# Layer 3 of a graph and expert network: the first normalisation moves to ScalarE, the routing bias to TensorE, and two VectorE steps go

## The reference

```
dw = (weight > 0.01) * 0.01 - (weight < -0.01) * 0.01
x = x + relu(adj @ (layernorm(x) @ dw) + bias)
xf = layernorm(x).reshape(-1, 128)
logits = xf @ router_w.T + router_b          # 32 experts
idx = argmax(logits)
out = relu(relu(xf @ W1[idx] + b1[idx]) @ W2[idx] + b2[idx])
x = x + out
```

## Time and profile before

| what | value |
|---|---|
| median of 3 runs | 2202.75 us |
| lowest and highest | 2199.62, 2203.97 us |
| the profiled execution's own time | 2199.14 us |
| its span | 2197.4 us |
| this stage, first row of L1763 to the end of the last send | 1785.1 to 2000.6 us |
| busy shares of the span: TensorE, VectorE, ScalarE, GpSimd | 77%, 56%, 38%, 35% |
| mean granted clock of TensorE | 0.866 of full speed |

### The profile page before, as it was taken

One profiled execution on the slowest core, in us unless ns is written; L12 is line 12 of the kernel. 1 busy time (PEld: TensorE's weight loads), 2 busy tenths in 40 slices (PEclk: granted clock), 3 DMA queues, 4 the chain that ended last, 5 costly groups with the idle time before them and its releaser, 6 DMA issues. The chain is left out here.

```text
span 2197.4 us, 44487 instructions
## 1 busy us (share of the span) xinstructions
PE 1691.7 (77%) x13042; PEld 1410.7 (64%) x13042; DVE 1234.2 (56%) x4542; ACT 824.8 (38%) x2531; POOL 764.8 (35%) x1118
## 2 busy tenths in 40 slices
PE   5567999987649966777777779935999957872996
PEld 4555777765639964566666657725999945661663
DVE  5673333349856756688888855512222248862543
ACT  2333444433336642344444434302655523330000
POOL 3430000013326745200000027773554424543565
PEclk8888999998879985799999989967999967665887
DMA  2100000001014420000000021114777752203331
GB/s 70 57 29 8 1 1 1 1 13 34 28 33 130 124 57 0 1 0 0 0 0 0 0 71 48 48 52 129 207 208 206 206 141 81 64 23 66 98 79 46
DMA packets 156776, 129.84 MB, mean 59 GB/s; under 512 B 27852, under 2 KB 131055, under 8 KB 156610
## 3 DMA queue, kind: packets, MB, share of 16 engines
q1 hardware_dynamic: 136130, 99.30, 16.6%
q0 software_dynamic: 13568, 25.90, 3.5%
q10 hardware_dynamic: 6912, 2.65, 0.6%
HBM read 96.51 MB, written 33.35 MB: 59 GB/s over the span
## 5 line engine op out<-in xcount | busy, mean ns | idle before, releaser
L1429 ACT ACTIVATE FEAT<-BANKS,EXP 128x128 f32<-128x128 f32 x544 | 155.0, 368 | 181.4 <-PE BANKS L1406 181.4
L1047 ACT ACTIVATE EXP<-BANKS,NEGMAX 128x128 f32<-128x128 f32 x512 | 139.0, 383 | 191.5 <-DVE NEGMAX L1059 191.5
L195 PE MATMUL BANKS<-ident,WA 128*128 128x128 f32 x256 | 62.8, 392 | 163.2 <-DVE WA L189 163.1
L1360 POOL DMA_INDIRECT scratch_made<-FEAT x136 | 130.2, 958 | 147.8 <-DVE FEAT L1489 144.8
L195 PEld LDWEIGHTS BANKS<-ident,WA 128*128 128x128 f32 x256 | 42.9, 199 | 174.2 <-DVE WA L189 136.8
L412 PE MATMUL BANKS<-FEAT,ident 128*128 128x256 f32 x588 | 150.0, 383 | 0.0
L1489 DVE TENSOR_TENSOR FEAT<-BANKS,B2BC 128x128 f32<-128x128 f32 x136 | 39.7, 292 | 194.5 <-PE BANKS L1415 194.5
L1406 PE MATMUL BANKS<-FEAT 128*128 128x128 f32 x1088 | 146.3, 278 | 2.4 <-DMA FEAT<-in_L_ffn_W1p 1.2
L1415 PE MATMUL BANKS<-AUX,FEAT 128*128 x1088 | 143.9, 275 | 0.4 <-ACT FEAT L1429 0.4
L1074 DVE RECIPROCAL WD<-BANKS 128x256 f32<-128x256 f32 x64 | 112.5, 1758 | 55.4 <-PE BANKS L1018 55.4
L1162 POOL DMA_INDIRECT scratch_sent<-FEAT,POS x128 | 123.7, 966 | 40.6 <-issue 37.8
(11 more groups left out here) (361 smaller groups left out, 4556.4 us busy)
## 6 DMA issues: line engine op xcount, KB each, us to landing
FEAT<-in_L_ffn_W1p SPq DMA_DIRECT2D x136, 256.0 KB
EXP<-in_L_ffn_W SPq DMA_DIRECT2D x128, 128.0 KB, 2.1
FEAT<-scratch_sent SPq DMA_DIRECT2D x136, 64.5 KB
STAGE<-in_adj SPq DMA_DIRECT2D x32, 256.0 KB, 3.0
EXP<-scratch_made SPq DMA_DIRECT2D x32, 256.0 KB
FEAT<-scratch_sent SPq DMA_DIRECT2D x96, 65.5 KB, 1.9
X<-in_x SPq DMA_DIRECT2D x16, 256.0 KB, 3.3
scratch_sent<-NONE SPq DMA_DIRECT2D x48, 65.5 KB, 3.9
```

Of the source, the lines that this page charges most:

```text
L195: last = pe.transpose(tile(ps, k), tile(src, k), ident[:])
L1047: last = act.activation(tile(EXS[:, par], 4 * k + n), tile(PS[j], c), ACT.Exp, bias=NEGMAX[:, par, 4 * k + n:4 * k + n + 1])
L1360: pool.indirect_dma_start(out=made2, out_offset=bass.IndirectOffsetOnAxis(ap=XI_I[:, t % R_IN, H:ROW2], axis=0), in_=YO[:, t % R_OUT, :], ...
L1429: last = act.activation(tile(HR[:, t % R_H], c), tile(PS[2 + t % 2], c), ACT.Gelu, bias=BT[:, c, t:t + 1])
```

## The change

The first normalisation of the stage is computed by ScalarE as x times a scale plus a shift; VectorE makes only the shift, minus mean times inverse deviation, for the four graphs of the group in one small instruction (shift1, L1714 in the new file). The router bias is loaded as one row and put into the logits' bank by a one-row matmul, as the graph bias already is, and the four logits matmuls add to it. The search for the greatest logit and for its index read the bank itself, and the comparison reads the index as the unsigned integer that it is. The bank of the logits is free again only when the index search has run (s.idx), no longer when the copy has (s.lg). GpSimd's dev now waits until ScalarE has read the RS of two groups before.

```diff
-        rb3 = lb("rb3", [P, E3])
+        rbrow = lb("rbrow", [1, E3])
+        NB3 = lb("NB3", [P, 2, G])
-        LG3 = lb("LG3", [P, 2, G, E3])
-        IDXG3 = lb("IDXG3", [P, 2, G, 8])
...
-                sp.dma_start(rb3[:], a["L3_ffn_router_b"].partition_broadcast(P)).then_inc(s.w, 16)
+                sp.dma_start(rbrow[:], a["L3_ffn_router_b"].rearrange("(o h) -> o h", o=1)).then_inc(s.w, 16)
...
                 def dev(i):
+                    reused(pool, s.xn, i, 2)
                     inverse_deviation(pool, i, i % 2, MV, RS, s.mv, s.var, s.rstd)
...
                 def logits(i):
                     pe.wait_ge(s.f, i + 1)
-                    reused(pe, s.lg, i, 1)
-                    for k in range(G):
-                        last = pe.matmul(PS[5][:, k * E3:(k + 1) * E3], tile(WF[:, i % 2], k), rw3[:], start=True, stop=True)
+                    reused(pe, s.idx, i, 1)
+                    pe.matmul(PS[5][:, 0:G * E3].rearrange("p (g e) -> p g e", g=G), ones[0:1, :],
+                              rbrow[:].unsqueeze(1).to_broadcast([1, G, E3]), start=True, stop=False, skip_group_check=True)
+                    for k in range(G):
+                        last = pe.matmul(PS[5][:, k * E3:(k + 1) * E3], tile(WF[:, i % 2], k), rw3[:],
+                                         start=False, stop=(k == G - 1), skip_group_check=True)
                     last.then_inc(s.lg_ps, 1)
...
             @block.scalar
+                def norm(i):
+                    act.wait_ge(s.shift1, i + 1)
+                    reused(act, s.x_ps, i, 2)
+                    for k in range(G):
+                        last = act.activation(tile(WA[:, i % 2], k), cols(X, G * i + k, H), ACT.Identity,
+                                              scale=RS[:, i % 2, 1, k:k + 1], bias=NB3[:, i % 2, k:k + 1])
+                    last.then_inc(s.xn, 1)
...
-                in_turn(NG, [(1, xT), (1, support), (3, norm2), (3, feat)])
+                in_turn(NG, [(1, norm), (1, xT), (1, support), (3, norm2), (3, feat)])
...
-                def norm(i):
+                def shift1(i):
                     v.wait_ge(s.rstd, i + 1)
-                    reused(v, s.x_ps, i, 2)
-                    normalise(v, i, i % 2, WA, MV, RS, 1, s.xn)
+                    reused(v, s.xn, i, 2)
+                    v.scalar_tensor_tensor(NB3[:, i % 2, :], MV[:, i % 2, :, 0], -1.0, RS[:, i % 2, 1, :], ALU.mult, ALU.mult
+                                           ).then_inc(s.shift1, 1)
...
-                    v.tensor_tensor(LG3[:, par], PS[5][:, 0:G * E3].rearrange("p (g e) -> p g e", g=G),
-                                    rb3[:].unsqueeze(1).to_broadcast([P, G, E3]), ALU.add).then_inc(s.lg, 1)
-                    wait_apart(v, s.lg, i + 1)
-                    for k in range(G):
-                        last = v.max(TOP3[:, par, k, :], LG3[:, par, k, :])
+                    for k in range(G):
+                        last = v.max(TOP3[:, par, k, :], PS[5][:, k * E3:(k + 1) * E3])
...
-                        last = v.max_index(IDX3[:, par, k, :], TOP3[:, par, k, :], LG3[:, par, k, :])
+                        last = v.max_index(IDX3[:, par, k, :], TOP3[:, par, k, :], PS[5][:, k * E3:(k + 1) * E3])
...
-                    v.tensor_copy(IDXG3[:, par], IDX3[:, par]).then_inc(s.idf, 1)
-                    v.wait_ge(s.idf, i + 1)
                     reused(v, s.rk, i, 3)
                     v.tensor_tensor(HOT[:, ring], iota32[:].unsqueeze(1).to_broadcast([P, G, E3]),
-                                    IDXG3[:, par, :, 0].unsqueeze(2).to_broadcast([P, G, E3]), ALU.is_equal).then_inc(s.hot, 1)
+                                    IDX3[:, par, :, 0].unsqueeze(2).to_broadcast([P, G, E3]), ALU.is_equal).then_inc(s.hot, 1)
...
-                in_turn(NG, [(1, norm), (3, shift), (0, combine), (0, stats), (6, place), (5, choice), (2, add), (4, top)])
+                in_turn(NG, [(1, shift1), (3, shift), (0, combine), (0, stats), (6, place), (5, choice), (2, add), (4, top)])
```

More of the change, by code:

```diff
@@ L1497, in program @@
                        "lg_ps lg top idx idf hot ms car rk rb pp pf pos neg posw dw dws g1 ctab got0 got1 got2 half used blank "
-                       "sent0 sent1 sent2 sent3 sent4 sent5 sent6")
+                       "shift1 sent0 sent1 sent2 sent3 sent4 sent5 sent6")
         s_got = (s.got0, s.got1, s.got2)
```

## The result

| | before | changed |
|---|---|---|
| median of 4 runs | 2201.18 us | 2222.54 us |
| lowest and highest | 2193.48, 2203.97 | 2208.90, 2224.49 |
| profiled execution, span | 2197.4 us | 2220.4 us |
| the stage, first weight step to the last send's start | 214.6 us | 244.4 us |
| its 13 full turns, logits to logits | 150.9 us | 178.1 us |

The ratio is 1.0102, with a 95% interval of 1.0068 to 1.0137: slower by about 1%, and outside the forecast range (2192 to 2212). The two spans differ by 23.0 us: the stage is 29.8 us longer, and the parts before and after it were 2.3 and 4.5 us shorter in this execution.

What follows compares the result with a forecast made beforehand. VectorE bounds the short turns, TensorE the long ones. Terms +5.8 + 0.7 - 2.7 - 1.5 = +2.3 us gave 2205.0 on the median; less 3.1 for the clock, forecast 2202.0 us, range 2192 to 2212.

Steps and rivals of the forecast that it cites:

- the clock term: TensorE's clock level in the stage's turns: one long turn fewer, taken as a choice, -3.1 us.
- more long turns: Rival, from bias through rank to logits: each additional long turn costs 3.9 us, giving 2209 or 2213; chance 0.17.
- Less work on VectorE: VectorE's turn 1.54 us shorter, so TensorE's rank no longer waits for HOT in full turns: -2.7 us.
- The bias matmul: New one-row matmul on TensorE before the logits, 0.28 to 0.52 us each, 16 blocks, not hidden: +5.8 us.
- ScalarE's normalisation: Four normalisations on ScalarE, 1.65 us: covered in full turns, uncovered in the first group, +0.7 us.
- The drain: After the last conv, three searches and two choices on VectorE get shorter on the way to POS: -1.5 us.
- Searches that read the bank: VectorE's search reading PSUM: not charged, from -0.03 to +0.05 us an instruction, eight in a turn.

Runs made afterwards that it cites:

- e2: Kernel before with only the one-row routing-bias matmul and the search on the bank; 2304.8 us against 2283.5 before, ratio 1.0085.
- e1: Changed kernel without its routing-bias matmul: VectorE copies the logits with the bias and the search reads that copy; 2279.4 us against 2283.5 before, ratio 0.9957.
- e5: Changed kernel with the routing bias on 128 rows, graph bias still on one; 2177.5 us against 2197.7 before, ratio 0.9914.
- e9: Changed kernel with the graph bias on 128 rows, routing bias still on one; 2176.4 us against 2200.9 before, ratio 0.9874.
- e14: Changed kernel with its one-row routing-bias matmul moved behind support, into TensorE's wait for norm2; 2259.1 us against 2284.9 before, ratio 0.9950.
- e13: Changed kernel with the routing bias on 128 rows and that matmul issued twice; 2276.2 us against 2284.9 before, ratio 1.0036.
- e8: Changed kernel with an unused 512-column, 128-row matmul added behind support, in TensorE's wait for norm2; 2193.0 us against 2197.7 before, ratio 0.9958.
- e3: Kernel before with only the first normalisation moved to ScalarE; 2271.6 us against 2283.5 before, ratio 0.9931.
- e10: Kernel before with only the graph bias put on 128 rows; 2189.0 us against 2200.9 before, ratio 0.9937.
- e6: Changed kernel with both the routing bias and the graph bias on 128 rows; 2165.6 us against 2197.7 before, ratio 0.9845.
- e11: e6 with the routing bias issued behind support, in TensorE's wait for norm2; 2162.9 us against 2200.9 before, ratio 0.9825.
- e12: e6 with both biases issued behind support, in TensorE's wait for norm2; 2163.4 us against 2200.9 before, ratio 0.9825.

## Why the prediction was wrong

**The step that failed is the clock term.** The prediction chose one long turn fewer, -3.1 us, because "less waiting is likelier to keep the high level than to lose it". The opposite came: all 13 full turns took 13.0 to 14.4 us, and together grew from 150.9 to 178.1 us, +27.2. That alone is more than the whole difference of the two spans (23.0 us). The mean granted clock over the 120 us fell from 0.70 to 0.57. The cause is the one-row bias matmul: e2, which has it and the search on the bank, has the whole loss (243.3 us), e1, which has neither, has mostly turns of 10.0, and e5 and e9 keep the search and have 10.2. e5, e9 and e14 show when it does harm: as one-row work, in a turn that already has 512 one-row columns, and in the stretch of work and not in the wait. How much of that is its rows and how much its length, e13 leaves open.

The rival **more long turns** had the side and the place right ("two blocks of one-row work now stand in a turn that already failed to lift the clock"), at a chance of 0.17. It priced one or two more long turns, 2209 to 2213; no full turn stayed short, and it was 2222.5. Six of the 13 are of a kind that the prediction didn't have, 13.04 us at a clock of 0.63. The range ended at 2212 for that reason. The prediction's own rows were enough to ask the question: in the long turn, TensorE was held by nothing but its ring at 0.50, so the one-row blocks and their place were what a new one would add to.

**The Trainium skill's rule** (TensorE: Matmul & The Clock Gate, section Why this matters for your kernels) would have continuous work release the clock. The runs agree in part. e8, which fills about 1 us of the gap, raises the mean clock from 0.57 to 0.72. But e5 has the same wait of 2.22 us in each turn and TensorE is busy for a smaller share of it (8.00 us of 10.22, against 10.50 of 12.72 and 12.45 of 14.67), and it has 0.83.

Of the other terms:

- **Less work on VectorE**: right. Busy time in a turn fell from 9.9 to 8.6 us, in the whole kernel by 21 us against 23 forecast. The waits for HOT in the full turns (-2.7 us) are gone. e3 (0.9931) and e9 against e10 (12.6 us) show a gain as long as the clock holds.
- **The bias matmul**: right in kind, priced at less than half. It takes 0.41 and 0.73 us at the two levels, and not 0.28 and 0.52, and with the idle time before its weight load and the next it costs 0.61 and 1.02. A quarter of the 512-column matmul leaves out what doesn't scale with columns. Six of the 16 ran at the high level and ten at the low one, some 14 us in place of 5.8, by my estimate from these rows. In the 13 full turns it is some 11 us; with the waits of 2.7 us gone, some 19 of the 27.2 us are left to the clock level, by the same estimate.
- **ScalarE's normalisation**: right. L1663 takes 485 ns an instruction, the block 1.65 us, and no full turn waits for it. In the first group it delays the transposes: from the start of the combine ahead of them to theirs it was 6.40 us before and is 7.13 after, +0.73, where +0.7 was forecast.
- **The drain**: the gain on VectorE came, the drain still got longer. The last two gaps from logits to logits took 6.81 and 7.36 us before, and 7.97 and 7.77 after: +1.6 us, where -1.5 was forecast. In the last gap, at the low level in both, the way over VectorE from the end of the logits to rank fell by 0.6 us, as forecast, and the bias matmul, which the prediction had booked elsewhere, added its 1.02.
- **Searches that read the bank**: nearly free. MAX8 went from 181 to 186 ns, FIND_INDEX8 from 186 to 191, and the comparison with the integers from 297 to 288. By the Trainium skill (VectorE: DVE Perf Modes, section The TRN2 errata) each would take 65 ns more, 120 cycles in place of 58 at 0.96 GHz. These rows show 5 ns.

The sum of what is known: turns +27.2, first group +0.7, drain +1.6, which is 29.5 of the stage's 29.8 us. The bias matmul's cost is inside these. The 6.8 us that the rest of the kernel gave back in this execution are not explained by any run.

**What stays open.** No run says why the level falls or rises where it does. No run separates rows from length: e13 comes near it, but is still 0.17 us shorter a turn, and its ratio doesn't bear out what its trace says; for the graph bias there is no such run at all.

## What to carry to other kernels

When a stage's turns fall into a short and a long kind at two clock levels, its time is set by which kind comes, and a term of a few tenths of a microsecond on TensorE decides more by that than by its own length; so price such an edit for both patterns, all short and all long, and let the range hold both. Put a bias that TensorE adds on all 128 rows (bias over 128, everywhere ones) and not on one: with both biases so, 2198 us became 2166 (e6), where the changed kernel with both on one row went from 2201 to 2222. Try it also where TensorE waits anyway; e11 and e12 came to 2163 from 2201, a step further that is within the noise. After each such gain look which cover has become thin; here ScalarE's normalisation was the next.

## What the runs showed of the hardware that was not expected

- The granted clock was lower with bias matmuls on one row than with the same columns on 128 rows. Both biases changed so, with nothing else, raised its mean from 0.57 to 0.84 and took the stage from 244.4 to 183.9 us (changed and e6). The 128-row form is also shorter, so this isn't shown to be the rows alone.
- A one-row matmul of 128 columns between 128-row ones takes 0.41 us at the high level and 0.73 at the low one; on 128 rows 0.22 and 0.42 (e5, e13). With what stands before the weight loads, the one-row form lengthens TensorE's list by 0.61 and 1.02 us. With 512 columns the matmul itself is 1.05 and 2.00 us on one row, 0.86 and 1.71 on 128 (e6).
- Moving the routing bias's one-row matmul by a few instructions, into a wait, took 43.6 us off the stage (e14).
- MAX8 and FIND_INDEX8 on 128x32 cost 5 ns more from PSUM than from SBUF (before and changed, 181 and 186 against 186 and 191 ns).
- The kernel before took 2201 us in some sessions and 2284 in others. By e1's trace this stage was not the cause: it began 56.5 us later, and what follows it took 29.9 us longer.
